# Cross-attention on one core: the inverse row sums copied to their heads' partitions by DMA instead of spread by matmuls, and the loop over tiles written out

## The chip, the core and the metric

The kernel runs on one core of a Trainium2 chip. TensorE (PE in the profile) multiplies matrices and writes PSUM banks; VectorE (DVE), ScalarE (ACT) and GpSimd (POOL) do the elementwise work; SyncE (SP) issues the transfers of the DMA engines. The metric is the time of one execution on the device, in microseconds (us); less is better.

## The reference

```python
# x (2, 2048, 640), ctx (2, 154, 1024): 77 text keys and 77 image keys a batch; 20 heads of 32
q    = split_heads(x @ Wq.T)
k, v       = split_heads(text @ Wk.T),  split_heads(text @ Wv.T)
k_ip, v_ip = split_heads(ip @ Wk_ip.T), split_heads(ip @ Wv_ip.T)
attend(q, k, v) = softmax(q @ k.T / sqrt(32)) @ v          # per head
out = merge_heads(attend(q, k, v)) + merge_heads(attend(q, k_ip, v_ip))
return out @ Wo.T + bo + x
```

There are two softmax branches (text and image), each with its own row sums, and their results are added before the output projection.

## The kernel before

The channels of everything are on the partitions, the rows of x on the free axis. The 4096 rows (2 batches of 2048) are cut into 16 tiles of N = 256. A tile has five **units**, g = 0 to 4; a unit is a group of four heads, 128 channels. So there are 80 units, counted 0 to 79. Every engine has its own program, and each runs through the same sequence of **stages**, one per unit u; in a stage an engine works on several units at once, each at another step. Semaphores tie them together; nothing but the order in which the code is written decides what stands behind what in an engine's queue.

In stage u TensorE does, in this order: the products for the maxima of unit u+1 (`max_scores`, bank a_ps) and their transposition (`turn_maxima`), between them the scores of unit u (`scores`, b_ps, for four heads j) and the projection of q of unit u+2 (`project_q`, q_ps, 15 matmuls, since float32 is split into a high and a low part); then the output projection of chunk u-10 (`project_out`, x_ps, 15 matmuls); the row sums of unit u (`row_sums`, sum_ps), for which all four exponentials of u must be there; and the values (`weigh_values`, pv_ps). Row sums of both branches and all five units of a tile gather in one bank, sum_ps: branch br of unit g stands, for head j, in rows 32 j + c and 32 j + 16 + c, with c = 2 g + br.

**The normalisation** of unit u-6 needs the inverse of these sums on each of the 32 partitions of a head. In the stage of g = 0 of the next tile ScalarE copies sum_ps to inv (`keep_sums`), VectorE inverts it and splits it into a high and a low part (`invert_sums`: inv, inv_hi, inv_parts). Per unit, TensorE then multiplies inv_parts by a selection matrix (`spread_inverse`, two matmuls of 256 columns into x_ps, one for each branch), and VectorE multiplies the bank by the kept values (`normalise`: scaled <- x_ps, pv_sb). GpSimd adds the two branches (scaled <- scaled), ScalarE rounds that to attn_hi, GpSimd subtracts to get attn_lo, and both are read by the output projection. As bank x_ps serves the spread, the projection and the bias in turn, the spread matmuls wait for ScalarE's y (`add_bias`). They stand between the row sums and the values; in stages of g = 0, where the new inverse has just come, behind the values.

ScalarE's order in a stage matters here and isn't changed:

```python
exp(u, 0); exp(u, 1); keep_pv(u.plus(-1))
# in stages of g == 0 also: keep_sums(before)
exp(u, 2); attn_high(norm)     # norm = u - 6
exp(u, 3); q_high(nxt); q_top(nxt); add_bias(chunk)
# in stages of g == 4 also: split_x(ahead)
```

GpSimd's order is: `add_branches(norm)`, `attn_low(norm)`, in stages of g = 1 `split_x` (x_lo), then `add_residual(chunk)`.

SyncE issues, in stage u: the maxima of u+1 (`maxima`, q_stack <- max_rows), a copy of q of u+2 (`third_block`, q_stack <- q_stack), the store of chunk u-10, the load of the residual for chunk u-5, and in stages of g = 2 the next x tile. Each waits for its data before it is issued, and whatever stands behind waits too.

The sequence of stages is written out for the first pair of tiles and for the last; the six pairs between them are a loop with a register as its counter (`stages`). After the last stage the last two tiles' projections are finished in an order of their own (`end_last_tiles`).

Of the kernel before, what the change touches and what calls it, by code (L numbers as in the profile page):

```python
# [37 lines left out]
P = 128  # L38
# [7 lines left out]
N = 256  # L46
# [54 lines left out]
def build(nc, x_d, ctx_d, wq_d, wk_d, wv_d, wo_d, bo_d, out_d):  # L101
    with ExitStack() as stack:
# [27 lines left out]
        low_rows = sbuf("low_rows", [P, 1])  # L130

        spread = sbuf("spread", [P, BRANCHES * GROUPS, GROUP, D], F32R)
# [19 lines left out]
        inv_hi = sbuf("inv_hi", [P, N], F32R)  # L152
        inv_parts = sbuf("inv_parts", [P, N], F32R)
# [22 lines left out]
        low_rows_done = sem("low_rows_done")  # L176
# [25 lines left out]
        inv_spread = sem("inv_spread")  # L202
# [10 lines left out]
        INV_STEPS = 3  # L213
# [32 lines left out]
        def _(sp):  # L246
# [64 lines left out]
            stages(emit)  # L311
            for n, c in enumerate(LAST_CHUNKS):
# [6 lines left out]
        def _(pool):  # L319
# [11 lines left out]
            nc.gpsimd.memset(spread[:].bitcast(F32), 0.0).then_inc(consts, 1)  # L331
            for step, row in enumerate((0, HALF)):
                pool.wait_ge(consts, 8 + step)
                nc.gpsimd.affine_select(out=spread[:], in_=spread[:], compare_op=ALU.not_equal, fill=1.0, base=-row,
                                        pattern=[[-1, BRANCHES * GROUPS], [-D, GROUP], [0, D]],
                                        channel_multiplier=1).then_inc(consts, 1)
# [47 lines left out]
        def _(act):  # L384
# [158 lines left out]
        def _(dve):  # L543
# [3 lines left out]
            dve.wait_ge(consts, 2)  # L547
            nc.vector.tensor_reduce(low_rows[:], ident[:].rearrange("p (j d) -> p j d", j=GROUP)[:, :, HALF:], AXIS.XY,
                                    ALU.add, negate=True).then_inc(low_rows_done, 1)
# [32 lines left out]
            def invert_sums(u):  # L582
# [3 lines left out]
                wait(dve, inv_spread, u.number())  # L586
# [418 lines left out]
```

## Time and profile before

| | |
|---|---|
| time, median of 3 runs | 714.46 us (714.28 to 715.46) |
| profiled execution, span from first to last instruction | 712.9 us |
| its own time beside the span | not given; the runs' median is 1.6 us above the span |
| TensorE busy | 679.8 us, 95% |
| VectorE, ScalarE, GpSimd busy | 441.4 us (62%), 493.3 us (69%), 224.0 us (31%) |
| mean granted TensorE clock | 0.988 of 2.4 GHz |
| moved by DMA | 57.44 MB, 26.0% of 16 engines' span |

Until about 80 us the weights are loaded and keys and values computed; the stages run from about 80 to 690 us. An engine's busy time says only how much it has to do; what an operation is worth is read from the order of time in a stage, and from the idle time ahead of an instruction, which the profile puts in brackets with the engine and line that ended it.

### The profile page before, as it was taken

The numbers are of one execution on the slowest core, as the hardware profiler recorded it, in microseconds if no ns is written. First come the engines' busy times: TensorE is split into PE (matmuls) and PEld (weight loads), VectorE is DVE, ScalarE is ACT, GpSimd is POOL, SyncE is SP. The second block draws the span as 40 slices with busy tenths as digits, with TensorE's granted clock in tenths as the row PEclk, the third lists the DMA queues.
The fourth block names the chain that finished last, engine by engine and source line by source line (L and its number), as shares of the span: only waits on it lengthen the run. The fifth ranks groups of instructions, "written<-read, shape, count | busy, mean of one in ns | idle before, by whom it ended". The sixth has DMA issues, their size and how long they took to land.

```text
span 712.9 us, 18904 instructions
## 1 busy us (share of the span) xinstructions
PE 679.8 (95%) x6514; PEld 560.9 (79%) x6514; DVE 441.4 (62%) x956; ACT 493.3 (69%) x1078; POOL 224.0 (31%) x261
## 2 busy tenths in 40 slices
PE   8959789999999999999999999999999999999997
PEld 8958566777877788778877887888778877887777
DVE  5786667665757565665656565655657575756633
ACT  3984687876767676767776777677767776776641
POOL 4020103243423324242424233242434233242333
PEclk9989899999999999999999999999999999999999
DMA  8940021313131312222121312112131313111211
GB/s 321 408 191 16 17 62 33 83 48 94 51 91 46 92 50 77 58 56 86 52 82 52 90 52 82 52 56 86 46 95 47 89 46 95 51 51 47 61 47 66
DMA packets 34690, 57.44 MB, mean 81 GB/s; under 512 B 4832, under 2 KB 27232, under 8 KB 34400
## 3 DMA queue, kind: packets, MB, share of 16 engines
q1 hardware_dynamic: 34656, 56.99, 26.0%
q8 instruction: 21, 0.34, 0.2%
q14 instruction: 13, 0.11, 0.0%
HBM read 35.34 MB, written 10.49 MB: 64 GB/s over the span
## 4 chain that ended last, share of the span: by engine, by line
PE 53%; ACT 30%; issue 10%; DVE 6%; ACTq 1%; POOL 0%; DVEq 0%
PE pv_ps L780 11%; ACT q_stack L397 9%; PE q_ps L711 9%; ACT probs L405 8%; PE x_ps L711 7%; PE b_ps L752 7%; PE a_ps L735 7%; PE x_ps L789 5%; PE sum_ps L769 5%; ACT y L428 3%; ACT q_hi L390 3%; ACT pv_sb L410 2%; ACT attn_hi L434 1%; DVE k_stack L631 1%; DVE k_stack L641 1%
## 5 line engine op out<-in xcount | busy, mean ns | idle before, releaser
L405 ACT ACTIVATE probs<-b_ps 77x512 f32<-77x512 f32 x320 | 181.1, 591 | 153.3 <-PE b_ps L752 151.7
L571 DVE TENSOR_REDUCE row_max<-a_ps 128x4 f32<-128x308 f32 x320 | 138.5, 474 | 86.6 <-PE a_ps L735 84.0
L562 DVE TENSOR_TENSOR q_stack<-q_ps,q_hi 32x256 fp32r<-32x256 f32 x320 | 134.3, 420 | 36.0 <-ACT q_hi L390 32.3
L397 ACT ACTIVATE q_stack<-q_hi 32x256 fp32r<-32x256 f32 x320 | 133.0, 416 | 10.0
L352 POOL TENSOR_TENSOR attn_lo<-scaled,attn_hi 128x256 fp32r<-128x256 f32 x80 | 58.9, 737 | 182.3 <-ACT attn_hi L434 182.3
L752 PE MATMUL b_ps<-q_stack,k_stack 98*77 98x256 f32 x640 | 115.6, 282 | 0.6 <-ACT probs L405 0.5
L735 PE MATMUL a_ps<-k_diag,q_hi 128*128 128x308 f32 x320 | 93.7, 333 | 7.5 <-DVE row_max L571 7.5
L598 DVE TENSOR_TENSOR scaled<-x_ps,pv_sb 128x512 f32<-128x512 f32 x75 | 51.9, 692 | 68.2 <-PE x_ps L789 67.6
L358 POOL TENSOR_TENSOR res<-y,res 128x256 f32<-128x256 f32 x70 | 51.1, 730 | 136.7 <-ACT y L428 136.7
L347 POOL TENSOR_TENSOR scaled<-scaled 128x256 f32<-128x256 f32 x80 | 58.5, 732 | 102.6 <-DVE scaled L598 102.5
L752 PEld LDWEIGHTS b_ps<-q_stack,k_stack 98*77 98x77 f32 x640 | 85.7, 147 | 2.3 <-ACT probs L405 1.3
L711 PE MATMUL q_ps<-x_lo,wq_hi 128*128 128x256 f32 x400 | 87.1, 284 | 0.0
L780 PE MATMUL pv_ps<-probs,v 128*32 128x256 f32 x1280 | 86.4, 388 | 0.0
L735 PEld LDWEIGHTS a_ps<-k_diag,q_hi 128*128 128x128 f32 x320 | 54.2, 188 | 35.9 <-issue 26.1
L769 PE MATMUL sum_ps<-probs,sum_one 128*32 128x256 f32 x1152 | 79.7, 390 | 1.1 <-ACT probs L405 1.1
L711 PE MATMUL q_ps<-x_hi,wq_hi 128*128 128x256 f32 x400 | 74.1, 283 | 6.5 <-POOL x_lo L341 6.3
L711 PE MATMUL q_ps<-x_hi,wq_lo 128*128 128x256 f32 x400 | 80.2, 298 | 0.0
L341 POOL TENSOR_TENSOR x_lo<-x_raw,x_hi 128x1280 fp32r<-128x1280 f32 x16 | 48.9, 3058 | 60.0 <-ACT x_hi L416 60.0
L711 PEld LDWEIGHTS q_ps<-x_lo,wq_hi 128*128 128x128 f32 x400 | 67.5, 193 | 0.0
L711 PE MATMUL x_ps<-attn_lo,wo_hi 128*128 128x256 f32 x365 | 66.7, 281 | 0.3 <-POOL attn_lo L352 0.3
L711 PE MATMUL x_ps<-attn_hi,wo_hi 128*128 128x256 f32 x365 | 66.7, 280 | 0.0
L711 PE MATMUL x_ps<-attn_hi,wo_lo 128*128 128x256 f32 x365 | 66.6, 280 | 0.0
(111 smaller groups left out, 939.3 us busy)
## 6 DMA issues: line engine op xcount, KB each, us to landing
x_raw<-x_in SPq DMA_DIRECT2D x16, 640.0 KB, 4.1
q_stack<-q_stack SPq DMA_DIRECT2D x80, 128.0 KB, 2.3
res<-x_in SPq DMA_DIRECT2D x75, 128.0 KB, 2.1
y_out<-res SPq DMA_DIRECT2D x75, 128.0 KB, 1.7
stage<-wk_in SPq DMA_DIRECT2D x6, 640.0 KB, 8.2
stage<-wv_in SPq DMA_DIRECT2D x6, 640.0 KB, 10.3
wq_raw<-wq_in SPq DMA_DIRECT2D x1, 1600.0 KB, 9.3
wo_raw<-wo_in SPq DMA_DIRECT2D x1, 1600.0 KB, 14.7
```

What stands on the lines that cost most here:

```text
L347: nc.gpsimd.tensor_tensor(scaled[:, s, 0:N], scaled[:, s, 0:N], scaled[:, s, N:2 * N], ALU.add).then_inc(attn_done, 1)
L352: nc.gpsimd.tensor_tensor(attn_lo[:, u.batch, u.g, :], scaled[:, u.slot, 0:N], attn_hi[:, u.batch, u.g, :].bitcast(F32), ALU.subtract).the ...
L397: done = nc.scalar.activation(q_stack[0:D, u.slot, j, :], q_hi[j * D:(j + 1) * D, u.slot, :].bitcast(F32), ACT.Copy)
L405: nc.scalar.activation(probs[0:KEYS, j, :], b_ps[j % 2][0:KEYS, :], ACT.Exp).then_inc(b_drained, 1)
L562: done = nc.vector.tensor_tensor(q_stack[D:2 * D, u.slot, j, :], q_ps[rows, 0:N], q_hi[rows, u.slot, :].bitcast(F32), ALU.subtract)
L571: nc.vector.tensor_reduce(row_max[:, u.slot, br, :, sub], bank[:, 0:BLK].rearrange("p (j n) -> p j n", j=GROUP), AXIS.X, ALU.max).then_inc ...
L598: nc.vector.tensor_tensor(scaled[:, u.slot, :], bank[:], pv_sb[:, u.g, :], ALU.mult).then_inc(scaled_done, 1)
L711: return nc.tensor.matmul(out, (lo if kind == 1 else hi)(k), (moving_lo if kind == 2 else moving_hi)(k), start=(n == 0), stop=(n == STEPS_ ...
L735: nc.tensor.matmul(a_ps[(u.c * A_ITEMS + k) % 2][:, 0:BLK], q_hi[:, u.slot, sub * P:(sub + 1) * P], k_diag[:, br, u.g, u.batch].rearrange( ...
L752: done = nc.tensor.matmul(b_ps[j % 2][0:KEYS, br * N:(br + 1) * N], k_stack[0:STACK, br, u.g * GROUP + j, u.batch, :], q_stack[0:STACK, u. ...
L769: nc.tensor.matmul(sum_ps[j * D:(j + 1) * D, 0:N], sum_first[:] if first else sum_one[:, D - 1 - c:2 * D - 1 - c], probs[:, j, br * N:(br ...
L780: done = nc.tensor.matmul(pv_ps[j * D:(j + 1) * D, br * N:(br + 1) * N], v[:, br, u.batch, h * D:(h + 1) * D], probs[:, j, br * N:(br + 1) ...
```

## The change

The inverse stays in float32 and isn't split. SyncE copies each of the two rows of a unit to the partitions of its head, with two DMAs per unit: 8 source rows of 1 KB (partitions row, row + 16, ...), each repeated 16 times, 128 KB in all, into a buffer inv_spread with two slots. The copy of a unit is issued a stage or more ahead of its normalisation. The two spread matmuls are gone, as are their wait for y and the selection matrix. In SyncE's queue the residual's load now stands ahead of the store, and is that of chunk u-6. On VectorE the normalisation of a tile's first unit moves behind the maxima of its stage. The loop over pairs of tiles is written out in all eight.

```diff
+        inv_spread = sbuf("inv_spread", [P, 2, BRANCHES * N])
+        inv_landed = [sem(f"inv_landed{s}") for s in range(2)]
...
-            pair(0)
-            with emit.engine.Fori(1, STEPS - 1) as t:
+            for t in range(STEPS):
                 pair(t)
-            pair(STEPS - 1)
@@ SyncE @@
+            def spread_inverse(u):
+
+                if u.g < 2:
+                    wait(sp, inv_done, u.tile(1, 1))
+                else:
+                    wait(sp, scaled_done, u.number(1, -1))
+                for br in range(BRANCHES):
+                    row = BRANCHES * u.g + br
+                    sp.dma_start(inv_spread[:, u.slot, br * N:(br + 1) * N],
+                                 inv[row::HALF, :].unsqueeze(1).broadcast_to([P // HALF, HALF, N])
+                                 ).then_inc(inv_landed[u.slot], DMA)
+
             def emit(u):
-                ahead = u.tile_plus(2)
+                ahead, norm = u.tile_plus(2), u.plus(1 - SPREAD_LAG)
+                if norm.exists() and norm.g > 2:
+                    spread_inverse(norm)
                 if u.plus(1).exists():
                     maxima(u.plus(1))
                 if u.plus(2).exists():
                     third_block(u.plus(2))
+                if u.plus(GROUPS - 1 - OUT_LAG).exists():
+                    load_residual(u.plus(GROUPS - 1 - OUT_LAG))
                 if u.plus(-OUT_LAG).exists():
                     store(u.plus(-OUT_LAG))
-                if u.plus(GROUPS - OUT_LAG).exists():
-                    load_residual(u.plus(GROUPS - OUT_LAG))
+                if u.g == 0 and u.tile_plus(-1).exists():
+                    spread_inverse(u.tile_plus(-1))
+                    spread_inverse(u.tile_plus(-1).plus(1))
+                if norm.exists() and norm.g == 2:
+                    spread_inverse(norm)
                 if u.g == 2 and ahead.exists():
                     wait(sp, x_lo_done, u.tile(1, 2))
                     sp.dma_start(x_raw[:], x_d[ahead.t, ahead.batch]).then_inc(x_loaded, DMA)
@@ SyncE, after the last stage @@
+            load_residual(LAST.plus(-1))
+            for g in range(GROUPS):
+                spread_inverse(LAST.plus(g))
@@ ScalarE @@
             def keep_sums(u):
 
                 wait(act, pv_ready, u.number(1, GROUPS))
-                wait(act, inv_done, u.tile(INV_STEPS))
+                before = u.tile_plus(-1)
+                if before.exists():
+                    last = before.plus(GROUPS - 1)
+                    wait(act, inv_landed[last.slot], last.uses_of_slot(SPREAD_DMAS))
+                    previous = before.plus(GROUPS - 2)
+                    wait(act, inv_landed[previous.slot], previous.uses_of_slot(SPREAD_DMAS))
@@ VectorE @@
-            def normalise(u, bank=x_ps):
-
-                wait(dve, inv_spread, u.number(1, 1))
+            def normalise(u):
+
+                wait(dve, inv_landed[u.slot], u.uses_of_slot(SPREAD_DMAS))
                 wait(dve, pv_drained, u.number(1, 1))
                 wait(dve, attn_lo_done, u.number(1, -1))
-                nc.vector.tensor_tensor(scaled[:, u.slot, :], bank[:], pv_sb[:, u.g, :],
+                nc.vector.tensor_tensor(scaled[:, u.slot, :], inv_spread[:, u.slot, :], pv_sb[:, u.g, :],
                                         ALU.mult).then_inc(scaled_done, 1)
@@ VectorE, emit @@
-                if norm.exists():
+                if norm.exists() and norm.g > 0:
                     normalise(norm)
                 if nxt.exists():
                     for k in range(MAXES):
                         max_piece(nxt, k)
                     max_turned(nxt)
+                if norm.exists() and norm.g == 0:
+                    normalise(norm)
                 if u.g == 0 and u.tile_plus(-1).exists():
                     invert_sums(u.tile_plus(-1))
@@ TensorE @@
             def project_out(c):
 
-                wait(pe, scaled_done, c.number(1, OUT_LAG - SPREAD_LAG))
+                wait(pe, y_done, c.number())
                 out_chunk(c, x_ps)
@@ TensorE, emit @@
                 row_sums(u)
-                if norm.exists() and norm.g > 0:
-                    spread_inverse(norm)
                 weigh_values(u)
-                if norm.exists() and norm.g == 0:
-                    spread_inverse(norm)
```

What the change does to the engines' streams is seen best where both kernels write the stages out, in the last pair of tiles. TensorE in a stage of g = 1, the kernel before: from the end of the output projection over the row sums to the next stage's first scores.

```order
L711 MATMUL x_ps<-attn_hi,wo_lo 128x256
L711 MATMUL x_ps<-attn_lo,wo_hi 128x256
L769 MATMUL sum_ps<-probs,sum_one 32x256 x8
L789 MATMUL x_ps<-inv_parts,spread 128x256 x2
L780 MATMUL pv_ps<-probs,v 32x256 x8
L735 MATMUL a_ps<-k_diag,q_hi 128x308 x2
L752 MATMUL b_ps<-q_stack,k_stack 77x256 x4
```

The same place in the changed kernel:

```order
L717 MATMUL x_ps<-attn_hi,wo_lo 128x256
L717 MATMUL x_ps<-attn_lo,wo_hi 128x256
L775 MATMUL sum_ps<-probs,sum_one 32x256 x8
L786 MATMUL pv_ps<-probs,v 32x256 x8
L741 MATMUL a_ps<-k_diag,q_hi 128x308 x2
L758 MATMUL b_ps<-q_stack,k_stack 77x256 x4
```

The two matmuls with the selection matrix are gone; nothing else in TensorE's stream moves.

VectorE, the kernel before, from the inversion in the stage of g = 0 (RECIPROCAL) over the stage of g = 1 (its maxima are the second and third row): a tile's first normalisation stands ahead of the maxima.

```order
L585 RECIPROCAL inv<-inv 128x256
L588 CAST inv_hi<-inv 128x256
L590 SCALAR_TENSOR_TENSOR inv_parts<-inv_hi,low_rows,inv 128x256
L562 TENSOR_TENSOR q_stack<-q_ps,q_hi 32x256 x4
L598 TENSOR_TENSOR scaled<-x_ps,pv_sb 128x512
L571 TENSOR_REDUCE row_max<-a_ps 128x4 x4
L579 CAST max_rows<-a_ps 16x128
```

VectorE in the changed kernel, the same place:

```order
L596 RECIPROCAL inv<-inv 128x256
L573 TENSOR_TENSOR q_stack<-q_ps,q_hi 32x256 x4
L582 TENSOR_REDUCE row_max<-a_ps 128x4 x4
L590 CAST max_rows<-a_ps 16x128
L603 TENSOR_TENSOR scaled<-inv_spread,pv_sb 128x512
L573 TENSOR_TENSOR q_stack<-q_ps,q_hi 32x256 x4
L603 TENSOR_TENSOR scaled<-inv_spread,pv_sb 128x512
```

The two steps behind the inversion are gone; the tile's first normalisation (scaled) stands behind the cast of the maxima, and ahead of q_stack; the second one is that of the stage of g = 2.

SyncE in the changed kernel, from the stage of g = 0 to the first row of g = 3 (before, each stage had max_rows, q_stack, y_out and res, with x_raw behind that of g = 2):

```order
L272 DMA y_out<-res 128x256
L294 DMA inv_spread<-inv 128x1x256 x4
L267 DMA q_stack<-max_rows 2x8x128
L283 DMA q_stack<-q_stack 32x1024
L278 DMA res<-x_in 128x256
L272 DMA y_out<-res 128x256
L294 DMA inv_spread<-inv 128x1x256 x4
L267 DMA q_stack<-max_rows 2x8x128
L283 DMA q_stack<-q_stack 32x1024
L278 DMA res<-x_in 128x256
L272 DMA y_out<-res 128x256
L317 DMA x_raw<-x_in 128x1280
```

The first four copies are those of the tile's units 0 and 1, behind the store of the stage of g = 0; the next four are those of unit 2, at the end of the stage of g = 1, and of unit 3, at the start of the stage of g = 2, ahead of the maxima. The two of unit 4 follow behind x_raw.

## Rows read from the trace of the kernel before

**Rows 1.** Stretches: length; busy PE, PEld, DVE, ACT, POOL; PEclk, DMA share, GB/s.
```profile
108.00:112.00 4.00, 4.00 (x39) 2.02 (x37) 3.41 (x7) 2.68 (x7) 0.00 (x0) 0.57 0.01 2
...
400.00:560.00 160.00, 157.22 (x1556) 128.87 (x1555) 97.76 (x215) 115.47 (x251) 55.39 (x64) 1.00 0.23 67
```

**Rows 2.** Timeline of TensorE: start, duration (us), what; idle before it and releaser.
```profile
491.93 1.07 PE L769 MATMUL sum_ps<-probs,sum_one 128*32 128x256 f32 x16
493.23 0.47 PE L789 MATMUL x_ps<-inv_parts,spread 128*128 128x256 f32 x2 [0.22 <-ACT y L428]
493.63 1.07 PE L780 MATMUL pv_ps<-probs,v 128*32 128x256 f32 x16
494.63 0.55 PE L735 MATMUL a_ps<-k_diag,q_hi 128*128 128x308 f32 x2
495.01 0.63 PE L752 MATMUL b_ps<-q_stack,k_stack 98*77 98x256 f32 x4
...
499.97 0.64 PE L769 MATMUL sum_ps<-probs,sum_first 128*32 128x256 f32 x8
...
500.86 1.05 PE L780 MATMUL pv_ps<-probs,v 128*32 128x256 f32 x16
501.84 0.51 PE L789 MATMUL x_ps<-inv_parts,spread 128*128 128x256 f32 x2
502.18 0.45 PE L735 MATMUL a_ps<-k_diag,q_hi 128*128 128x308 f32 x2
...
507.53 1.07 PE L769 MATMUL sum_ps<-probs,sum_one 128*32 128x256 f32 x16
...
534.18 0.55 PE L735 MATMUL a_ps<-k_diag,q_hi 128*128 128x308 f32 x2
```

**Rows 3.** Groups by line: count, busy us, mean ns, idle before.
```profile
L598 DVE TENSOR_TENSOR scaled<-x_ps,pv_sb 128x512 f32<-128x512 f32 x75 | 51.9, 692 | 68.2 <-PE x_ps L789 67.6
```

**Rows 4.** Timeline of VectorE.
```profile
498.38 1.73 DVE L585 RECIPROCAL inv<-inv 128x256 f32<-128x256 f32 x1
...
502.73 0.69 DVE L598 TENSOR_TENSOR scaled<-x_ps,pv_sb 128x512 f32<-128x512 f32 x1
...
505.63 0.28 DVE L579 CAST max_rows<-a_ps 16x128 fp32r<-16x128 f32 x1 [0.46 <-PE a_ps L741]
```

**Rows 5.** Timeline of ScalarE.
```profile
505.04 0.41 ACT L434 ACTIVATE attn_hi<-scaled 128x256 fp32r<-128x256 f32 x1
505.35 0.58 ACT L405 ACTIVATE probs<-b_ps 77x512 f32<-77x512 f32 x1
```

**Rows 6.** Timeline of GpSimd.
```profile
503.50 0.73 POOL L347 TENSOR_TENSOR scaled<-scaled 128x256 f32<-128x256 f32 x1 [1.50 <-DVE scaled L598]
...
506.22 2.93 POOL L341 TENSOR_TENSOR x_lo<-x_raw,x_hi 128x1280 fp32r<-128x1280 f32 x1
```

**Rows 7.** Timeline of SyncE: duration is that of the issue.
```profile
502.04 0.35 SPq L279 DMA_DIRECT2D y_out<-res  x1
...
505.94 0.70 SPq L274 DMA_DIRECT2D q_stack<-max_rows  x1
```

**Rows 8.** DMA issues on the page: KB each, median us from issue to landing.
```profile
x_raw<-x_in SPq DMA_DIRECT2D x16, 640.0 KB, 4.1
q_stack<-q_stack SPq DMA_DIRECT2D x80, 128.0 KB, 2.3
res<-x_in SPq DMA_DIRECT2D x75, 128.0 KB, 2.1
```

**Rows 9.** Timeline of TensorE in the first two tiles.
```profile
106.77 0.41 PE L735 MATMUL a_ps<-k_diag,q_hi 128*128 128x308 f32 x1 [1.67 <-DVE row_max L571]
...
116.49 1.07 PE L769 MATMUL sum_ps<-probs,sum_one 128*32 128x256 f32 x16 [0.26 <-ACT probs L405]
```

**Rows 10.** The chain that ended last, at the end of the kernel.
```profile
693.35 0.23 PE sum_ps L789 x2
...
708.11 0.13 PE a_ps L842
```

More of the change, by code:

```diff
@@ L211, in build @@
         stored = sem("stored")
-        INV_STEPS = 3
+        SPREAD_DMAS = BRANCHES * DMA
         K_ITEMS = BRANCHES * GROUPS
@@ L330, in _ @@
             nc.gpsimd.memset(k_diag[:, 1].bitcast(F32), 0.0).then_inc(zeroed, 1)
[L331 to L336, printed above, removed]
             def split_x(u):
@@ L585, in invert_sums @@
                 nc.vector.reciprocal(inv[:], inv[:]).then_inc(inv_done, 1)
-                wait(dve, inv_spread, u.number())
-                wait(dve, inv_done, u.tile(INV_STEPS, 1))
-                nc.vector.tensor_copy(inv_hi[:], inv[:]).then_inc(inv_done, 1)
-                wait(dve, inv_done, u.tile(INV_STEPS, 2))
-                nc.vector.scalar_tensor_tensor(out=inv_parts[:], in0=inv_hi[:].bitcast(F32), scalar=low_rows[:],
-                                               in1=inv[:], op0=ALU.mult, op1=ALU.add).then_inc(inv_done, 1)
-            def normalise(u, bank=x_ps):
-                wait(dve, inv_spread, u.number(1, 1))
+            def normalise(u):
+                wait(dve, inv_landed[u.slot], u.uses_of_slot(SPREAD_DMAS))
                 wait(dve, pv_drained, u.number(1, 1))
                 wait(dve, attn_lo_done, u.number(1, -1))
-                nc.vector.tensor_tensor(scaled[:, u.slot, :], bank[:], pv_sb[:, u.g, :],
+                nc.vector.tensor_tensor(scaled[:, u.slot, :], inv_spread[:, u.slot, :], pv_sb[:, u.g, :],
                                         ALU.mult).then_inc(scaled_done, 1)
@@ L690, in _ @@
             finish_last(0)
-            normalise(LAST, sum_ps)
+            normalise(LAST)
             for n in (1, 2):
@@ L694, in _ @@
             for g in (1, 2, 3):
-                normalise(LAST.plus(g), sum_ps)
+                normalise(LAST.plus(g))
                 if g + 2 < GROUPS:
                     finish_last(g + 2)
-            normalise(LAST.plus(4), sum_ps)
+            normalise(LAST.plus(4))
             for n in range(GROUPS, 2 * GROUPS):
@@ L783, in weigh_values @@
                 done.then_inc(pv_ready, 1)
-            def spread_matmuls(u, bank):
-                for br in range(BRANCHES):
-                    sel = spread[:, BRANCHES * u.g + br].rearrange("p j d -> p (j d)")
-                    done = nc.tensor.matmul(bank[:, br * N:(br + 1) * N], sel, inv_parts[:], start=True, stop=True)
-                done.then_inc(inv_spread, 1)
-            def spread_inverse(u):
-                if u.g == 0:
-                    wait(pe, inv_done, u.tile(INV_STEPS, INV_STEPS))
-                wait(pe, scaled_done, u.number())
-                wait(pe, y_done, u.number(1, 1 + SPREAD_LAG - OUT_LAG))
-                spread_matmuls(u, x_ps)
             def project_out(c):
-                wait(pe, scaled_done, c.number(1, OUT_LAG - SPREAD_LAG))
+                wait(pe, y_done, c.number())
                 out_chunk(c, x_ps)
@@ L822, in end_last_tiles @@
             def end_last_tiles():
-                def spread_last(g):
-                    if g == 0:
-                        pe.wait_ge(inv_done, LAST.tile(INV_STEPS, INV_STEPS))
-                    else:
-                        pe.wait_ge(scaled_done, LAST.number(1, g))
-                    spread_matmuls(LAST.plus(g), sum_ps)
                 def grow(k):
@@ L849, in chunk @@
                     if n == 0:
-                        pe.wait_ge(scaled_done, LAST.number())
+                        pe.wait_ge(y_done, LAST_CHUNKS[0].number())
                     elif n == 1:
@@ L872, in emit @@
             def emit(u):
-                nxt, norm, chunk = u.plus(1), u.plus(-SPREAD_LAG), u.plus(-OUT_LAG)
+                nxt, chunk = u.plus(1), u.plus(-OUT_LAG)
                 def find_max(k):
@@ L940, in _ @@
             pe.wait_ge(k_lo_done, K_ITEMS)
-            pe.wait_ge(consts, 10)
+            pe.wait_ge(consts, 7)
             first = Unit(0, 0)
```

15 lines of the change are left out of this document (removed).

## The prediction

> **What bounds the kernel now.** I read the table by stretch first. From 400 to 560 us TensorE is busy for 157.22 of 160 us, at full clock (1.00); VectorE is busy for 97.8 and ScalarE for 115.5 [rows 1]. So in the middle of the run an operation costs time if it stands in TensorE's stream, or if it makes that stream wait. The same stream unit by unit [rows 2]: one tile is five units, and from its first unit (a_ps at 494.63) to the first of the next (534.18) it is 39.55 us. The unit of g = 0 takes 502.18 - 494.63 = 7.55 us; the other four take (39.55 - 7.55) / 4 = 8.00 on average.
>
> **What the removed matmuls cost.** In an ordinary unit the row sums start at 491.93 and the values at 493.63: 1.70 us. In the g = 0 unit nothing stands between them: 499.97 to 500.86, 0.89 us [rows 2]. The difference, 0.81 us, is the pair of spread matmuls with their wait for ScalarE's y (0.22 us in the row of 493.23). In the g = 0 unit the pair stands behind the values and costs 501.84 to 502.18, 0.34 us. Without them the units are 7.55 - 0.34 = 7.21 and 8.00 - 0.81 = 7.19 us, a tile 7.21 + 4 x 7.19 = 35.97 instead of 39.55: 3.6 us less. I take 3.5, as the wait for y is not equally long everywhere. There are 75 normalisations in the main stream [rows 3], so 75 pairs: units 5 to 79. Units 10 to 74 are 13 tiles: 13 x 3.5 = 45.5 us. Units 5 to 9 (no output projection yet) and 75 to 79 (less and less of it) don't wait for y so regularly; between 0.34 and 0.81 I take 0.45: 10 x 0.45 = 4.5. Gross gain: **50.0 us**.
>
> **What takes the matmuls' place.** VectorE's normalisation must now wait for a transfer, and for a tile's first unit it stands behind the maxima of its stage, not ahead of them. Let P be a tile's first unit; its sums are inverted in unit P+5, and its normalisation is in unit P+6 (g = 1). I follow that in the stage that starts in the trace at 494.63 (P+5) and 502.18 (P+6). In the changed kernel P+6 starts at 494.63 + 7.21 = 501.84.
> - SyncE: the inverse is ready at 498.38 + 1.73 = 500.11 [rows 4], but the copies are queued behind the store, which waits for GpSimd's residual add and ends its issue at 502.04 + 0.35 = 502.39 [rows 7]. No row shows an issue of this form: 0.35 us is that of the store, 0.70 that of the other copy with a pattern of three dimensions. I take 0.70: the second of a unit's two copies starts at 503.1.
> - Landing: 128 KB takes 2.1 us from HBM and 2.3 between partitions; 640 KB takes 4.1 [rows 8]. A 128 KB copy just behind another one is delayed by it: 512 KB more cost 2.0 us, so 128 KB about 0.5. Hence 2.3 to 2.8: landed at 505.4 to 505.9. The bounds are 2.1 (505.2) and 4.1 (507.2).
> - VectorE: the cast of the maxima ends at 505.63 + 0.28, 3.73 us after the unit's start [rows 4], so at 505.57. The normalisation starts at about 505.7 and ends 0.69 later, 506.4.
> - GpSimd starts 0.08 us later (502.73 + 0.69 to 503.50) and adds the branches in 0.73 [rows 4, 6]: 507.2. ScalarE has attn_hi of this unit ahead of its last exponential, in both kernels; that exponential starts 0.31 us after attn_hi and takes 0.58 [rows 5]: 508.1.
> - TensorE: the row sums need all exponentials. They are due 507.53 - 502.18 = 5.35 us into the unit [rows 2], at 507.19.
> So TensorE waits 0.9 us in each g = 1 unit, and each 0.1 us by which the copy lands after 505.6 is added in full. I take 1.05. What is queued behind: on VectorE q_low of the next unit but one, on ScalarE the last exponential, q_hi and y. 14 such units (11, 16, ... 76) cost 14.7 us. In unit 6 there is no projection to cover it: there the sums already wait 0.26 us for the exponential [rows 9]. The wait will be over 2 us, and the only gap of such a kind in the trace (1.67 us, [rows 9]) is followed by a granted clock of 0.57 for 4.00 us [rows 1]; I take 3.5 us for unit 6.
>
> **SyncE.** Each unit gets two more issues, 1.4 us, in a queue that is idle most of a unit: hidden, except behind the g = 1 unit. There GpSimd goes attn_lo (after attn_hi, done about 508.4), the x_lo split of 2.93 us, residual add 0.73 [rows 6]: 512.1. Then store 0.35 and four copies of 0.70: 515.3. Only then the transfer of the next maxima is issued. The scores that read it come 0.4 us into the unit after (495.01 - 494.63 in [rows 2]), 501.84 + 7.19 + 1.05 + 7.19 + 0.4 = 517.7; at 2.3 us it lands at 517.6. The margin is thin; I take 0.1 us per tile, 1.4 in all. The load of the residual now stands ahead of the store and is issued one unit later, so it waits for a store of the unit before instead of the one just issued. That frees SyncE for the copies; by itself it is worth nothing, and the load is still four units ahead of its use.
>
> **Other edits, costed at nothing.** The cast and the split of the inverse (VectorE, 0.8 us per tile) go away beside TensorE's work. Memsets and selects on GpSimd at the start lie under the loads. The written-out loop takes out register instructions; TensorE's gap-free g = 0 unit was 7.55 in the loop, so little is left to win there. What could be lost is time in which instructions have not arrived; the first and last pair of tiles are written out in the kernel before too, and units there take no longer than in the loop.
>
> **The end.** Five pairs go at 0.23 us each [rows 10], 1.15 us. TensorE works some 15 us from the first of these pairs (693.35) to its end (708.11), partly on just this data. In return each of the last five units needs a copy, and units 2 to 4 may only issue theirs when a buffer of two is free: three rounds of about 0.7 issue + 2.5 landing + 0.7 normalising = 12 us after the last inverse. That fits under the 15, closely. I take +0.3 us.
>
> Sum: 50.0 - 14.7 - 3.5 - 1.4 - 0.3 = 30.1. On the profiled execution that is a span of 712.9 - 30.1 = 682.8; the runs' median is 714.46, 1.6 above that span, so **684.5 us**.
>
> **How many engines carry a copy.** The rows say 2.1 to 2.3 us for 128 KB, whatever the side. The Trainium skill (DMA: Bandwidth & Descriptors, "Why a DMA increments its semaphore by 16 and not by 1") speaks against it: the number of engines is the largest up to 16 that divides the slowest dimension of both patterns. The source here has 8 rows, so 8 engines would carry it, each with twice the bytes. By that rule, an estimate, a copy lands some 0.5 us later, and with the two queued 1.0: 14 x 0.5 to 1.0, 691 to 698 us. No row of before shows a copy of this shape; the sum above does without it.
>
> **The rivals.**
> - A, the normalisation is hidden anyway (no wait in the g = 1 units): 684.5 - 14.7 - 3.5 - 1.4 = 665. Against it stands the order: VectorE's cast, GpSimd and ScalarE in series are 2.5 us from 505.57, with 1.6 us of cover. Chance 0.05.
> - B, late landing: the copies or the maxima's transfer come 0.4 to 1.3 us later than I take it (slower patterns, 0.93 us of engine time instead of 0.5, four in a row behind the g = 1 unit). 14 x 0.4 to 1.3: 690 to 703. The bound of 4.1 us [rows 8] gives 507.2, 1.5 us later than 505.7: 705. Chance 0.19.
> - C, the clock: if each wait of 1 us drops TensorE to 1.2 GHz as the gap of 1.67 did, 4.00 us at 0.57 cost 4.00 x 0.43 = 1.7 us; 14 x 1.7 = 24: 708. The gaps of up to 0.5 us elsewhere were not followed by it. Chance 0.12.
> - D, slower than before: a copy takes so long that the wait eats the 3.5 us of a tile. The forecast is used up at 30.1 / 14 = 2.15 us more per tile: a landing at 505.7 + 2.15 = 507.9, 4.8 us after its issue, where 128 KB took at most 2.3 and 640 KB 4.1. At 6 us it would be 14 x 3.4 over the forecast, 732. Chance 0.05.
> - E, starved instruction fetch in the written-out loop: 0.1 to 0.4 us a unit, 690 to 715. Chance 0.03.
> The forecast as worked out (680 to 688) keeps 0.56.
>
> **The numbers.** The range goes from 677 to 706: it holds the forecast, B and part of C and E, and leaves A, D and the rest of C out. Its own range is 680 to 688. Faster by over 0.2% (about what this kernel's measurement can tell): everything but D, a sliver of E: 0.93; within 0.2% 0.02; slower 0.05.
>
> **What would show it.** Row sums directly followed by values, 0.9 us apart, and ordinary units of 7.2 us; once per tile, in the g = 1 unit, row sums waiting about 1 us for the exponential, behind it attn_hi waiting for GpSimd and that for VectorE; copies landing within 2.3 to 2.8 us; granted clock 1.00 from 140 us on. I am wrong if the g = 1 wait is absent or over 2 us, if scores wait for the maxima's transfer, or if ordinary units are not near 7.2 us.

## The result and the profile after

The changed kernel takes **757.05 us**, median of 4 runs (755.55 to 757.59). The kernel before took 714.83 beside it (714.28 to 715.46). The ratio is 1.0587, 95% interval 1.0572 to 1.0602: 5.9% slower. The forecast was 684.5 us, faster. The profiled execution has a span of 755.7 us (712.9 before) and a mean granted clock of 0.948 (0.988).

The table by stretch, columns as in [rows 1]:

```profile
400.00:560.00 160.00, 143.45 (x1411) 119.66 (x1404) 92.77 (x193) 104.92 (x231) 53.83 (x61) 0.96 0.37 98
```

TensorE was busy for 157.22 of these 160 us before, now for 143.45, at 0.96 of full clock instead of 1.00. DMA's share went from 0.23 to 0.37. The page's groups show what TensorE and the others waited for (the last fields: idle before, then releaser):

```profile
L758 PE MATMUL b_ps<-q_stack,k_stack 98*77 98x256 f32 x640 | 120.3, 291 | 19.4 <-DMA q_stack<-max_rows 18.5
L775 PE MATMUL sum_ps<-probs,sum_one 128*32 128x256 f32 x1152 | 86.7, 417 | 38.3 <-ACT probs L414 38.3
L603 DVE TENSOR_TENSOR scaled<-inv_spread,pv_sb 128x512 f32<-128x512 f32 x80 | 71.2, 890 | 36.0 <-DMA inv_spread<-inv 33.1
L419 ACT ACTIVATE pv_sb<-pv_ps 128x512 f32<-128x512 f32 x80 | 47.4, 592 | 61.4 <-DVE scaled L603 59.9
```

Row sums wait for the exponential, scores for the maxima's transfer, VectorE's normalisation for the copies. The normalisation takes 890 ns on average, not 692 [rows 3]. The fourth row is new too: ScalarE's keep_pv (PSUM to pv_sb) waits for a normalisation. pv_sb has five slots, so unit u-1 may only be kept when u-6 has been normalised.

Now one tile closely, TensorE's timeline (as [rows 2]; rows of the stages of g = 1 and 2):

```profile
537.21 1.28 PE L775 MATMUL sum_ps<-probs,sum_one 128*32 128x256 f32 x16 [2.26 <-ACT probs L414]
538.24 1.95 PE L786 MATMUL pv_ps<-probs,v 128*32 128x256 f32 x16
540.12 0.88 PE L741 MATMUL a_ps<-k_diag,q_hi 128*128 128x308 f32 x2
...
549.59 0.67 PE L758 MATMUL b_ps<-q_stack,k_stack 98*77 98x256 f32 x4 [1.14 <-DMA q_stack<-max_rows]
```

The chain of waits through the same stages names who was late, in order of time:

```profile
529.98 0.67 SPq L294
530.65 0.04 issue
530.69 3.79 DMA inv_spread<-inv
534.48 0.02 issue
534.50 0.70 DVE scaled L603
...
537.47 2.86 POOL x_lo L350
540.34 1.15 POOL res L367
541.49 0.02 issue
541.50 0.35 SPq L272
...
545.39 3.96 DMA q_stack<-max_rows
```

Both long bars are transfers. A 128 KB copy takes 3.79 us from its issue to its landing; the small transfer of the maxima, queued behind four such copies, takes 3.96. ScalarE's timeline between them:

```profile
535.29 0.60 ACT L419 ACTIVATE pv_sb<-pv_ps 128x512 f32<-128x512 f32 x1 [3.89 <-DVE scaled L603]
535.78 0.58 ACT L414 ACTIVATE probs<-b_ps 77x512 f32<-77x512 f32 x1
536.26 0.41 ACT L448 ACTIVATE attn_hi<-scaled 128x256 fp32r<-128x256 f32 x1
536.57 0.59 ACT L414 ACTIVATE probs<-b_ps 77x512 f32<-77x512 f32 x1
```

Two exponentials stand behind the keep_pv that waits for the normalisation, and the row sums (537.21) behind the second of them. GpSimd and VectorE around x_lo:

```profile
537.43 2.91 POOL L350 TENSOR_TENSOR x_lo<-x_raw,x_hi 128x1280 fp32r<-128x1280 f32 x1
540.29 1.19 POOL L367 TENSOR_TENSOR res<-y,res 128x256 f32<-128x256 f32 x1
```

```profile
537.46 1.72 DVE L573 TENSOR_TENSOR q_stack<-q_ps,q_hi 32x256 fp32r<-32x256 f32 x4 [2.26 <-ACT q_hi L399]
539.21 1.68 DVE L603 TENSOR_TENSOR scaled<-inv_spread,pv_sb 128x512 f32<-128x512 f32 x1
540.92 0.86 DVE L582 TENSOR_REDUCE row_max<-a_ps 128x4 f32<-128x308 f32 x2
```

The normalisation of the tile's second unit takes 1.68 us instead of 0.69 and ends 0.55 us after x_lo. Then the clock, from the table by stretch:

```profile
538.20:541.00 2.80, 2.80 (x23) 1.50 (x16) 2.71 (x5) 1.46 (x4) 2.80 (x2) 0.50 0.21 47
541.00:549.00 8.00, 7.45 (x76) 6.13 (x74) 4.95 (x12) 5.40 (x12) 3.33 (x5) 0.98 0.47 115
```

After the wait of 2.26 us the granted clock is 0.50, the 1.2 GHz level; 0.98 in the next stretch. In half-microsecond slices it is below 1.00 from 537.5 to 541.5, which makes some 3.4 us at 0.50 and costs 1.7 us of work. It does not fall after the wait of 1.14 us. A wait of this length does not always bring the fall: of the ten waits for the exponential between 240 and 640 us (2.24 to 2.90 us), seven did and three (2.24, 2.27 and 2.49) did not, and in those three tiles the clock fell with the wait for the maxima that came next (2.07 to 2.10 us).

**The account per tile.** I measure a tile from the row sums of one g = 0 unit to the next: before 39.44 to 39.71, mean 39.60 (11 tiles between 160 and 640 us); after 41.44 to 43.23, mean 42.03 (10 tiles). From 160 to 640 us, 11.4 tiles, TensorE waits 26.3 us for exponentials, 15.7 for maxima's transfers and 1.3 for row_max: 3.8 us a tile. The clock falls about once a tile, at 1.7 us each, 21.7 us in this time: 1.9 a tile. Together 5.7, so about 36.3 us of work remain in a tile.

### The profile page after: what moved, and what is told of

The parts are those of the page before. It is cut to its first block, busy times and chain, and to the rows that moved or that the text cites. A ratio compares the mean times of both kernels' runs of the same rounds, so it can differ in the third digit from the quotient of the medians.

```text
span 755.7 us, 16493 instructions
## 1 busy us (share of the span) xinstructions
PE 670.6 (89%) x6354; PEld 560.9 (74%) x6354; DVE 446.2 (59%) x923; ACT 490.8 (65%) x1078; POOL 224.2 (30%) x258
## 4 chain that ended last, share of the span: by engine, by line
PE 40%; DMA 17%; ACT 15%; POOL 11%; SPq 9%; DVE 4%; issue 4%; ACTq 0%; DVEq 0%; POOLq 0%
PE q_ps L717 9%; DMA inv_spread<-inv 9%; PE x_ps L717 7%; SPq L294 7%; DMA q_stack<-max_rows 7%; PE b_ps L758 6%; PE sum_ps L775 5%; POOL x_lo L350 5%; PE pv_ps L786 4%; PE a_ps L741 4%; ACT q_stack L406 4%; ACT probs L414 4%; POOL res L367 3%; DVE scaled L603 2%; PE b_ps L889 1%
## 5 line engine op out<-in xcount | busy, mean ns | idle before, releaser
L758 PE MATMUL b_ps<-q_stack,k_stack 98*77 98x256 f32 x640 | 120.3, 291 | 19.4 <-DMA q_stack<-max_rows 18.5
L775 PE MATMUL sum_ps<-probs,sum_one 128*32 128x256 f32 x1152 | 86.7, 417 | 38.3 <-ACT probs L414 38.3
L758 PEld LDWEIGHTS b_ps<-q_stack,k_stack 98*77 98x77 f32 x640 | 88.1, 153 | 25.0 <-issue 22.5
L741 PE MATMUL a_ps<-k_diag,q_hi 128*128 128x308 f32 x320 | 96.9, 344 | 8.2 <-DVE row_max L582 8.2
L367 POOL TENSOR_TENSOR res<-y,res 128x256 f32<-128x256 f32 x70 | 57.2, 817 | 131.8 <-ACT y L442 131.8
L786 PE MATMUL pv_ps<-probs,v 128*32 128x256 f32 x1280 | 93.7, 414 | 0.0
L603 DVE TENSOR_TENSOR scaled<-inv_spread,pv_sb 128x512 f32<-128x512 f32 x80 | 71.2, 890 | 36.0 <-DMA inv_spread<-inv 33.1
L419 ACT ACTIVATE pv_sb<-pv_ps 128x512 f32<-128x512 f32 x80 | 47.4, 592 | 61.4 <-DVE scaled L603 59.9
L775 PEld LDWEIGHTS sum_ps<-probs,sum_one 128*32 128x32 f32 x1152 | 32.6, 115 | 64.7 <-ACT probs L414 42.6
L786 PEld LDWEIGHTS pv_ps<-probs,v 128*32 128x32 f32 x1280 | 45.2, 120 | 33.7 <-issue 10.2
```

The source lines that it names most:

```text
L367: nc.gpsimd.tensor_tensor(res[:, c.g, :], y[:, c.slot, :], res[:, c.g, :], ALU.add).then_inc(y_added, 1)
L603: nc.vector.tensor_tensor(scaled[:, u.slot, :], inv_spread[:, u.slot, :], pv_sb[:, u.g, :], ALU.mult).then_inc(scaled_done, 1)
L741: nc.tensor.matmul(a_ps[(u.c * A_ITEMS + k) % 2][:, 0:BLK], q_hi[:, u.slot, sub * P:(sub + 1) * P], k_diag[:, br, u.g, u.batch].rearrange( ...
L758: done = nc.tensor.matmul(b_ps[j % 2][0:KEYS, br * N:(br + 1) * N], k_stack[0:STACK, br, u.g * GROUP + j, u.batch, :], q_stack[0:STACK, u. ...
L775: nc.tensor.matmul(sum_ps[j * D:(j + 1) * D, 0:N], sum_first[:] if first else sum_one[:, D - 1 - c:2 * D - 1 - c], probs[:, j, br * N:(br ...
L786: done = nc.tensor.matmul(pv_ps[j * D:(j + 1) * D, br * N:(br + 1) * N], v[:, br, u.batch, h * D:(h + 1) * D], probs[:, j, br * N:(br + 1) ...
```

## The experiments

Times are medians, ratios to the kernel before on the same chip (714.3 to 715.2 us). "Tile" is the mean over 10 to 12 tiles, measured as above.

**unroll_only.** The kernel before with the loop over pairs of tiles written out.

```diff
-            pair(0)
-            with emit.engine.Fori(1, STEPS - 1) as t:
+            for t in range(STEPS):
                 pair(t)
-            pair(STEPS - 1)
```

> The kernel before with nothing changed but the loop over tiles written out. Theory 1 (all of the loss comes from the copies: waits for them and for what is queued behind them): no change, 713 to 716 us. Theory 2 (the written-out loop starves an engine of instructions): over 720 us, with idle time of TensorE or another engine that no other engine ends.

709.32 us, 0.9919 (0.9902 to 0.9935); tile 39.22. TensorE's waits from 240 to 640 us: before, 21 for ScalarE's y, 4.4 us in all; here none. The page counts 16777 instructions instead of 18904. Neither expectation foresaw a gain. With the loop y was late, and writing it out is worth 0.38 us a tile, 5 to 6 us in all; which of the loop's instructions made y late is not shown.

**no_copies.** The changed kernel without the copies and the waits for them: it normalises by ones, which leaves out the division by the row sums.

```diff
-                for br in range(BRANCHES):
-                    sp.dma_start(inv_spread[...], inv[row::HALF, :]...).then_inc(inv_landed[u.slot], DMA)
...
-                wait(dve, inv_landed[u.slot], u.uses_of_slot(SPREAD_DMAS))
```

> The changed kernel without its 160 copies and without the waits for them: the normalisation multiplies by a buffer of ones, so the softmax isn't normalised; every other instruction stays. Theory 1: the matmuls' 50 us are all won, less the wait in the g = 1 units that the order alone makes (cast, normalisation, pv_sb, two exponentials and attn_hi in series: about 1.1 us, 14 times) and perhaps a lower clock behind it: 676 to 700 us, no wait for q_stack<-max_rows. Theory 2 (loop, order of the rest of SyncE's queue): it stays over 730 us.

694.94 us, 0.9726 (0.9707 to 0.9744); tile 38.05. Its waits on TensorE between 240 and 640 us (total us, times, longest):

```profile
PE sum_ps L767 <- ACT probs L410: 10.6, 10, 1.3
PE a_ps L733 <- DVE row_max L573: 4.5, 10, 0.5
```

So the copies cost 757.05 - 694.94 = 62 us. Without them each tile still waits 1.03 us for the exponential and 0.46 for row_max.

**straight_copy and sixteen_rows.** The same number of copies of 128 KB, but of other rows: the spreading of a head's row to its partitions is left out. The changed kernel reads 8 rows, each 16 times.

```diff
-                                 inv[row::HALF, :].unsqueeze(1).broadcast_to([P // HALF, HALF, N])
+                                 inv[:, :]                                                             # straight_copy
+                                 inv[0::P // HALF, :].unsqueeze(1).broadcast_to([HALF, P // HALF, N])  # sixteen_rows
```

> The changed kernel with copies of the same size, number and place, but of all 128 partitions as they stand instead of 8 rows repeated 16 times, so the output is not normalised rightly. If the pattern is what makes a copy slow (8 source rows, so fewer DMA engines, and an address pattern of three dimensions), the issue falls towards 0.35 to 0.5 us, the normalisation's wait of 1.25 us in a g = 1 unit goes away, the wait for the maxima (1.1 to 2.1 us) mostly too, and the time falls by 30 to 55 us to 700 to 727. If the number of bytes and of transfers in one queue is what costs, it stays at 745 to 760.

> The changed kernel with 16 source rows (partitions 0, 8, 16, ...), each repeated 8 times, in place of 8 rows repeated 16 times; same bytes, same count of pieces of 1 KB, same three dimensions, but not the right rows, so the output is not normalised rightly. Theory E (number of DMA engines: it follows from the slowest dimension, 8 before, 16 here): as the straight copy, 705 to 715 us, landing 2.2 us. Theory R (repeating a row, or the third dimension, is slow in itself): within 10 us of the changed kernel, 745 to 765.

708.97 us, 0.9913 (0.9886 to 0.994), tile 38.91; and 712.57 us, 0.9962 (0.9945 to 0.9979), tile 39.08. The DMA issues on the two pages (KB, us to landing):

```profile
inv_spread<-inv SPq DMA_DIRECT2D x160, 128.0 KB, 2.2
```

```profile
inv_spread<-inv SPq DMA_DIRECT2D x160, 128.0 KB, 2.5
```

Sixteen rows repeated 8 times land nearly as quickly as 128 rows. The same bytes from 8 rows repeated 16 times cost 44 us more. Between 240 and 640 us TensorE waits for the maxima in neither version, and the wait for the exponential is 1.8 us a tile instead of 2.3. How fast the copies move, from the table by stretch, while hardly anything else is under way, in the changed kernel and then in sixteen_rows:

```profile
406.00:408.50 2.50, 1.17 (x10) 0.96 (x9) 0.69 (x1) 0.76 (x2) 0.72 (x1) 1.00 0.44 95
```

```profile
426.50:428.50 2.00, 1.91 (x17) 1.70 (x15) 0.89 (x2) 0.10 (x1) 0.12 (x1) 1.00 0.78 190
```

Half the rate, at little more than half the share of the engines: by these rates 128 KB take 1.4 us and 0.7 us (estimates).

The medians of the pages hide the place that matters. The second copy of a tile's first unit, on which the g = 1 wait hangs, lands 3.79 to 4.41 us after its issue in the changed kernel (mean 3.9, 11 tiles), but 3.12 to 3.64 in sixteen_rows and 3.04 to 3.85 in straight_copy too (mean 3.4 in both, 12 tiles each). The pattern is worth 0.5 us there. The rest comes with the place in the queue: the copy of q, the residual's load, the store and the unit's first copy are issued in the 2.4 us before. Which of them delays it is not shown.

**maxima_first.** In SyncE's queue the copies of units 3 and 4 go behind the transfer of the maxima.

```diff
+                if u.plus(1).exists():
+                    maxima(u.plus(1))
                 if norm.exists() and norm.g > 2:
                     spread_inverse(norm)
-                if u.plus(1).exists():
-                    maxima(u.plus(1))
```

> The changed kernel, in SyncE's queue the copies of the units of g = 3 and 4 moved behind the transfer of the next maxima instead of ahead of it. Theory 1 (the maxima land late since four copies are issued ahead of them): TensorE's wait for q_stack<-max_rows in the g = 3 unit (1.1 to 2.1 us a tile) and the clock drop behind it go away; the wait for the exponential in the g = 1 unit (2.26) stays: 725 to 738 us. Rival (the maxima's transfer is slow wherever it stands, as the DMA engines are busy): the wait stays over 1 us and the time over 745.

728.8 us, 1.019 (1.0167 to 1.0213); tile 40.03. The wait for the maxima is gone (28 us less), the one for the exponential stays: 24.2 us in 10 tiles.

**first_early.** The copies of a tile's first unit are issued ahead of the third block, the residual's load and the store.

```diff
+                if u.g == 0 and u.tile_plus(-1).exists():
+                    spread_inverse(u.tile_plus(-1))
                 if u.plus(2).exists():
                     third_block(u.plus(2))
...
                 if u.g == 0 and u.tile_plus(-1).exists():
-                    spread_inverse(u.tile_plus(-1))
                     spread_inverse(u.tile_plus(-1).plus(1))
```

> The changed kernel with one step moved: the two copies for a tile's first unit are issued ahead of the third block, the residual's load and the store. Theory: the normalisation of that unit no longer waits for its copies (1.25 us at 534.50) but for its place behind the maxima, and the row sums of g = 1 wait about 1 us as without copies instead of 2.26: 14 x 1.25 = 17 us less, and less loss of clock: 732 to 742 us. The scores still wait for the maxima in the stages of g = 2 or 3. Rival: the waits for the maxima take over what is gained, since their transfers stand behind the same store and burst: 748 to 757.

742.62 us, 1.0395 (1.0365 to 1.0426); tile 40.95. TensorE's timeline over one tile:

```profile
402.33 1.07 PE L776 MATMUL sum_ps<-probs,sum_one 128*32 128x256 f32 x16 [1.03 <-ACT probs L415]
406.60 0.41 PE L742 MATMUL a_ps<-k_diag,q_hi 128*128 128x308 f32 x1 [0.44 <-DVE row_max L583]
...
414.80 1.11 PE L759 MATMUL b_ps<-q_stack,k_stack 98*77 98x256 f32 x4 [2.11 <-DMA q_stack<-max_rows]
```

The exponential's wait is that of no_copies to the hundredth (in seven of nine tiles), so what was above 1.03 us came from the late copy. The wait for the maxima grew to 2.1 us: both theories hold in part, and the result lies 0.6 us above the first's range.

**exps_first.** ScalarE, in the stage of g = 1: all four exponentials ahead of keep_pv and attn_hi.

```diff
                 exp(u, 0)
                 exp(u, 1)
+                if u.g == 1:
+                    exp(u, 2)
+                    exp(u, 3)
```

> The changed kernel, on ScalarE in stages of g = 1 all four exponentials ahead of pv_sb and attn_hi. Theory 1: the row sums no longer wait for the chain from the late copy (2.26 us, 14 times, and the clock drop behind it); the values may wait for pv_sb instead (it comes 0.6 us after the normalisation, 1.7 us ahead of attn_hi's end before). Time 757 - 14 x (1 to 3) = 715 to 743 us; the wait for the maxima (1.1 to 2.1 us) stays. Rival (the wait only moves to the values): within 6 us of 757.

754.64 us, 1.0556 (1.0537 to 1.0575): the first theory failed. The time is in the rival's range, but the wait moved only a little to the values, and most of it to the row maxima:

```profile
406.56 1.07 PE L791 MATMUL pv_ps<-probs,v 128*32 128x256 f32 x16 [0.23 <-ACT pv_sb L419]
409.15 0.74 PE L722 MATMUL q_ps<-x_hi,wq_hi 128*128 128x256 f32 x4 [0.38 <-DVE q_stack L578]
411.87 0.63 PE L746 MATMUL a_ps<-k_diag,q_hi 128*128 128x308 f32 x1 [1.51 <-DVE row_max L587]
```

VectorE's timeline has the reason: the second normalisation, beside x_lo, takes 2.18 us and holds up row_max. The clock still falls, after seven of the ten waits of 1.5 us for row_max, and in the other three tiles at the wait for the maxima; each fall costs 1.7 us.

```profile
409.12 2.18 DVE L608 TENSOR_TENSOR scaled<-inv_spread,pv_sb 128x512 f32<-128x512 f32 x1
411.33 0.86 DVE L587 TENSOR_REDUCE row_max<-a_ps 128x4 f32<-128x308 f32 x2
```

**nc_exps, nc_xlo, nc_order.** On no_copies (all normalise by ones): exps_first's edit alone, a move of x_lo alone, and both. The move:

```diff
                 if norm.exists():
                     add_branches(norm)
+                if u.g == 2 and ahead.exists() and u.number() != 2:
+                    split_x(ahead)
+                if norm.exists():
                     attn_low(norm)
-                if u.g == 1 and ahead.exists() and not (u.fixed and u.number() == 1):
-                    split_x(ahead)
```

> The changed kernel without the copies and the waits for them (it normalises by ones), and in the stages of g = 1 ScalarE's four exponentials stand ahead of keep_pv and attn_hi. Theory 1 (order on ScalarE): the wait of the row sums for the exponential, 1.03 us per tile without copies (694.94 us), goes: 694.9 - 13 x 1.03 = 681, and the wait for row_max (0.46) stays. Theory 2 (the slow normalisation is what is late, 1.7 instead of 0.69 us beside GpSimd's x_lo): the wait only moves from the row sums to the scores, as it did with the copies in place; time 690 to 697, the wait for row_max grows to 1 us or more per tile.

> The changed kernel without the copies and the waits for them (it normalises by ones), with GpSimd's x_lo moved one stage on, from behind attn_lo of g = 1 to behind the addition of the branches of g = 2. Theory (VectorE's normalisation is slowed by x_lo running beside it): the normalisation of 1.7 us in each tile falls to 0.7, the wait for row_max (0.46) goes, and the exponential behind attn_hi is 1 us less late, so that its wait (1.03) nearly goes too: 694.9 - 13 x 1.2 to 1.5 = 675 to 679 us. Rival (ScalarE's order alone makes the wait): normalisation faster or not, the row sums still wait 1 us: 689 to 695.

> The kernel without copies (normalisation by a buffer of ones, 694.9 us), with the exponentials first in stages of g = 1, and on GpSimd the x_lo split moved to stages of g = 2, behind the branches' add and ahead of attn_lo. If the 1.03 us wait of the row sums is ScalarE's order and the 0.46 us wait behind the normalisation of 1.71 us (0.69 elsewhere) is VectorE and GpSimd in each other's way while x_lo runs, both go: 14 x 1.8 = 25 us less, 667 to 674 us, which is the 50 us of the removed matmuls. If the 1.71 us has another cause, it stays and the time is 676 to 685.

nc_exps: 689.5 us, 0.9652 (0.9624 to 0.968), tile 37.82; the wait for the exponential is gone, the one for row_max has grown from 0.46 to 1.34, as the second theory has it. nc_xlo: 686.16 us, 0.9605 (0.9577 to 0.9633), tile 37.33, between its two expectations; its normalisations in the middle of the run (ns min/median/max):

```profile
L594 DVE TENSOR_TENSOR scaled<-inv_spread,pv_sb x53: 691/693/694, 244.3 to 637.4; 128x512 f32<-128x512 f32 x53
```

None is slow, and row_max is in time, but the exponential's wait of 1.03 us stays. nc_order: **668.22 us**, 0.9347 (0.933 to 0.9364), tile 36.33:

```profile
400.00:560.00 160.00, 160.00 (x1653) 136.32 (x1652) 103.99 (x226) 124.73 (x272) 62.90 (x72) 1.00 0.26 73
```

TensorE has no gap here. The first edit alone is worth 5.4 us, the second 8.8, both 26.7: each wait hides behind the other.

**exps_and_xlo, all_four.** With the copies in place: exps_first's edit with the move of x_lo; and these with maxima_first and first_early.

> The changed kernel with ScalarE's four exponentials first in g = 1 and x_lo moved to g = 2; SyncE's queue stays as the change has it. If both late copies and late maxima cost their waits on their own, the time lies between the version with all four edits (675.4) and the changed kernel (757.05): waits for the maxima of 1.1 to 2.1 us in one stage per tile stay, with the clock lost behind them: 700 to 730 us. Rival: without the late store (x_lo no longer ahead of the addition whose store stands ahead of the four copies) the maxima's transfer comes in time by itself: 676 to 685.

> The changed kernel with four edits: copies of g = 3 and 4 behind the maxima's transfer, those of a tile's first unit right behind the maxima in the stage of g = 0 (ahead of the q copy and the store), exponentials first in stages of g = 1, x_lo split moved to g = 2. Theory 1 (all the loss is waits that these four orders make): 668 to 690 us, no wait over 0.5 us a tile, clock 0.98 or more. Rival (the copies' load on the DMA engines delays whatever else is transferred): 695 to 725 us, with waits for q_stack<-max_rows or inv_spread left.

exps_and_xlo: 745.23 us, 1.0432 (1.0402 to 1.0462), tile 40.89. It lies above both expectations. SyncE's timeline (durations are those of the issues) and TensorE's:

```profile
410.07 3.45 SPq L294 DMA_DIRECT2D inv_spread<-inv  x4
413.56 1.12 SPq L267 DMA_DIRECT2D q_stack<-max_rows  x1
```

```profile
417.82 0.67 PE L764 MATMUL b_ps<-q_stack,k_stack 98*77 98x256 f32 x4 [2.16 <-DMA q_stack<-max_rows]
```

The store is earlier than in the changed kernel (12.4 us after the tile's first row sums, not 13.9), yet the scores wait longer: TensorE is no longer late itself, so it meets the late maxima in full. TensorE's waits from 240 to 700 us sum to 28.9 us, 2.6 a tile, and the clock falls in seven of ten tiles between 240 and 640 us, 1.2 us a tile (tiles without a fall take 39.8 to 40.1 us, with it 41.4 to 41.7); some 0.8 of the 4.6 us above nc_order's tile I have not traced.

all_four: **675.36 us**, 0.9442 (0.9429 to 0.9455), 5 runs; tile 36.51; 5.6% faster than the kernel before.

```profile
400.00:560.00 160.00, 158.63 (x1627) 135.16 (x1631) 103.65 (x224) 124.43 (x271) 62.17 (x70) 1.00 0.42 110
```

The two reorderings of SyncE are thus worth 70 us once the others are made. Over nc_order remain 7.1 us: 0.18 x 14 = 2.5 in the tiles, and 4.2 from the last tile's first row sums to TensorE's last matmul (51.47 against 47.29 us), where a wait of 2.4 us for VectorE's last residual sums is new.

## Why the prediction was wrong, step by step

- **The removed matmuls: the mechanism was right, the size too large.** Forecast 3.5 us a tile. Matmuls and loop together give 39.60 - 36.33 = 3.27, of which the loop is 0.38 and the matmuls 2.89. The waits for y in the pair's 0.81 us were the loop's: with the loop written out they are gone while the pairs are still there (unroll_only). Over the whole run nc_order is 41.1 us below unroll_only, where the forecast had 50.0. Without any wait the time was forecast at 665 (rival A); nc_order takes 668.2, so near only because the loop's gain, which the forecast did not have, makes up for part of that.
- **The loop written out, costed at nothing: wrong by 5 to 6 us.** I looked only at the gap-free g = 0 unit, and not at what made y late in the others.
- **The g = 1 wait, 1.05 us: the order was right, the landing wrong.** With no copy to wait for it is 1.03 us (no_copies); worked out was 0.9, taken 1.05. The step that failed is "landing 2.3 to 2.8". The second copy was issued 1.2 us into the stage (530.69, stage from 529.50), as forecast (1.26), but landed 3.79 us later. Two terms in this were mis-sized. The transfers issued just before it delay the copy more than the 0.5 us I gave to the first copy alone: with a quick pattern it still lands after 3.4 us (sixteen_rows, straight_copy). The pattern of 8 rows adds the other 0.5 us. The normalisation began 1.1 us later than forecast, and the wait became 2.3 us. Even so the path was incomplete: I followed ScalarE's attn_hi, not its keep_pv, which stands one exponential further ahead and waits for the same normalisation. From the normalisation's end to attn_hi are 1.07 us (535.19 to 536.26), forecast 0.81. So 0.9 + 1.1 + 0.3 = 2.3.
- **SyncE's thin margin, 0.1 us: this step failed too.** The transfer of the maxima is issued 5.27 us into the stage (545.39, stage from 540.12), forecast 5.22. Its landing was taken as 2.3 and is 3.96, behind four copies (3.83 to 4.04 in 11 tiles): 1.0 to 2.1 us of wait, 15.7 us in 11.4 tiles instead of 1.1. first_early and exps_and_xlo show it at 2.1. In sixteen_rows, where the four copies move twice as fast, this wait is absent between 240 and 640 us.
- **The clock.** Rival C priced a fall at 1.7 us, and that is its price here. I gave it 0.12 as a case by itself. It came on top of B and D's late landings, since they made the waits longer: 1.9 us in a tile, about 26 us in all.
- **Not foreseen: the normalisation beside x_lo.** It used to read x_ps (PSUM) and pv_sb; both its inputs are now in SBUF. The one that falls beside x_lo takes 1.67 to 1.71 us in ten of ten tiles, where q_stack, which reads PSUM and SBUF, keeps its 1.72 for four beside the same x_lo. nc_xlo shows that x_lo is the cause: with it moved away, all normalisations take 0.69. That the operand's place decides it is argued, not shown by a run: in the kernel before no normalisation ran beside x_lo. The Trainium skill (SBUF — State Buffer, "SBUF: two separate sides") says that VectorE with two SBUF inputs and a GpSimd operation that reads SBUF exclude each other for a whole instruction. The trace agrees: the normalisation ends 0.55 us after x_lo, and GpSimd's residual add beside it takes 1.19 instead of 0.73.
- **How many engines carry a copy.** I left this out of the sum, since no row showed the shape. sixteen_rows against the changed kernel is that test: the same bytes from 16 rows repeated 8 times, not 8 repeated 16 times, and 44 us less. The share of the engines (0.44 against 0.78) is down with the rate (95 against 190 GB/s), although copies are queued. Sixteen engines that were only slowed, by reading the same row 16 times, would keep their share; which engine moves a packet the trace does not show. By the rule of the Trainium skill (DMA: Bandwidth & Descriptors, "Why a DMA increments its semaphore by 16 and not by 1") a source of 8 rows is carried by 8 engines. The trace agrees. The estimate by this rule, 691 to 698, moved the forecast the right way but stayed below 714.8, since it priced the wait once a tile and left out the queue behind the copies and the clock. Rival B's 0.93 us of engine time for a copy stands in no row; by the rates above it is 1.4.
- **Unit 6: forecast 3.5 us, too small.** The row sums waited 3.62 us there (119.26), and the clock was 0.50 from 120 to 124 us. The tile from 109.00 us takes 38.91, before 34.57: 4.3 us more, forecast 1.2 more.
- **The end: forecast +0.3, in fact more.** From the last tile's first row sums to its last matmul TensorE needs 55.65 us instead of 50.52; by the forecast it would have been 0.8 less. The last tile has the g = 1 wait and the wait for the maxima as the others do. In all_four, without these, it is 4.2 us over nc_order, so the copies do not hide under TensorE's last 15 us; which of the three rounds is late I have not traced.

The sum again, in spans: 755.7 us instead of 682.8 is 72.9 us too long. The 13 tiles from 147.91 to 695.61 us take 547.70 us, before 514.45: 33.3 more, where 13 x (3.5 - 1.05 - 0.1) = 30.6 less was forecast, so 63.8 us lie there. The tile with unit 6 holds 3.1 and the end 5.9. Rival D had the mechanism (a landing 4.8 us after issue makes it slower), with the copies alone as its cause; in fact 3.8 us were enough, since the landing, the maxima's transfer and the clock went together.

## What to carry to other kernels

A broadcast by DMA is priced by the shape of its pattern, by what is issued just ahead of it and by what is queued behind it: put several copies behind, not ahead of, the small transfer that the next stage waits for, and take a landing time from a row in the same place of the queue, not from the median. When an instruction is made to wait, follow each engine's queue for everything that waits for its result, buffer slots included, since several waits can hide behind one another and then only fall together. When both inputs of a VectorE operation are in SBUF, look at what GpSimd does at that time.

## What the runs showed of the hardware

- The same 128 KB between partitions, medians of 160 copies: landing 2.2 us from 128 rows, 2.5 from 16 rows repeated 8 times. As the second copy of a tile's first unit: 3.4 us for both, 3.9 from 8 rows repeated 16 times, means of 11 or 12 tiles.
- Issues behind copies of 8 rows get slower: four of these take 3.45 to 4.09 us, the first of them 0.67, and the maxima's issue behind them 1.12 instead of 0.70. Four copies of 16 rows take 2.50 to 3.81 us, and the maxima's issue behind them 0.70.
- VectorE's 128x512 product of two SBUF operands took 0.69 us, and 1.67 to 1.71 beside GpSimd's x_lo; the normalisation and the residual's addition were both longer where they met.
- TensorE's clock fell to 0.50 for some 3.4 us after a wait of 2.26 us, after 1.5 us in exps_first in seven of ten tiles, and after 2.1 us in exps_and_xlo in some tiles and not in others. It did not fall after 1.14 or, in nc_exps, after 1.34 in each tile (its clock is 1.00 from 400 to 560 us).
